# A second attention loop of four units, a ring of two tiles, and operands split first and transposed by DMA

## The reference

```python
x = x + tanh(g_xattn[0]) * xattn0(layernorm(x), ctx)   # 8 heads of 64
x = x + tanh(g_ffn[0])   * expert_choice(layernorm(x)) # 16 experts, sinkhorn, top 32 of 64 tokens
x = x + tanh(g_xattn[1]) * xattn1(layernorm(x), ctx)   # 16 heads of 64
x = x + tanh(g_ffn[1])   * routed(layernorm(x))        # top 2 of 8 experts by each row's first token

def xattn(x, context):
    q, k, v = x @ Wq, context @ Wk, context @ Wv       # split into heads
    attn = softmax(einsum('bhsd,bhld->bhsl', q, k) * 64 ** -0.5)
    return einsum('bhsl,bhld->bhsd', attn, v) @ Wo + bo
```

## Time and profile before

| | us |
|---|---|
| median of 3 runs | 2118.46 (2116.81 to 2119.19) |
| profiled execution, its own time | 2109.9 |
| its span | 2108.1 |
| first attention, first to last projection of queries | 18.9 to 337.4 |
| selection | 355.6 to 486.0 |
| experts | 487 to 1325.4 |
| second attention, first to last projection of queries | 1331.6 to 1968.7 |
| routed layer | 1992.4 to 2108.1 |

### The profile page before, as it was taken

How to read it: one execution, slowest core, us unless ns; L and a number is a source line. 1 busy time by engine, 2 the same in 40 slices (tenths; PEclk the granted TensorE clock), 3 DMA queues, 4 the chain that set the end, 5 groups by cost and what they waited for, 6 DMA issues and landing times. The chain is left out here.

```text
span 2108.1 us, 97301 instructions
## 1 busy us (share of the span) xinstructions
PE 1857.5 (88%) x40785; PEld 1450.6 (69%) x40785; DVE 1582.0 (75%) x3646; ACT 1541.3 (73%) x2701; POOL 671.8 (32%) x920
## 2 busy tenths in 40 slices
PE   5899997877999999999999999687878878889898
PEld 4788886533666666666666676676767767778687
DVE  6899987697888888888888877666656656666654
ACT  4688885666999998989898988466656656677543
POOL 4687776321000000000000000344444444444555
PEclk9999998996999999999999999799989989999899
DMA  6644444591000000000000010366556555533233
GB/s 167 116 94 92 90 95 90 189 368 47 12 15 13 14 12 14 12 14 12 14 14 14 9 48 2 80 112 123 123 96 120 114 108 108 115 72 61 64 106 115
DMA packets 313482, 162.50 MB, mean 77 GB/s; under 512 B 236686, under 2 KB 295990, under 8 KB 313142
## 3 DMA queue, kind: packets, MB, share of 16 engines
q1 hardware_dynamic: 312294, 156.77, 32.5%
q10 hardware_dynamic: 848, 0.71, 0.2%
HBM read 62.07 MB, written 36.57 MB: 47 GB/s over the span
## 5 line engine op out<-in xcount | busy, mean ns | idle before, releaser
L1655 DVE TENSOR_TENSOR h<-g,h 128x1024 f16<-128x1024 f32 x256 | 313.5, 1225 | 138.3 <-ACT h L1587 137.7
L244 PEld LDWEIGHTS psE<-ew,h 128*128 128x128 f16 x6144 | 351.0, 98 | 55.9 <-issue 40.1
L244 PE MATMUL psE<-ew,h 128*128 128x128 f16 x6144 | 365.1, 219 | 12.8 <-DVE eo L1665 6.0
L1582 ACT ACTIVATE g<-psH,eb1T 128x512 f32<-128x512 f32 x512 | 330.3, 680 | 30.9 <-PE psH L244 24.5
L751 POOL TENSOR_TENSOR Ph<-E,Ph 128x512 f16<-128x512 f32 x192 | 222.5, 1159 | 355.0 <-ACT Ph L671 355.0
L671 ACT ACTIVATE QK<-psQK 128x512 f32<-128x512 f32 x216 | 128.8, 596 | 223.9 <-PE psQK L554 223.8
L1587 ACT ACTIVATE h<-g 128x1024 f16<-128x1024 f32 x256 | 270.6, 1057 | 8.1
L1728 POOL MEMSET rbias<- 64x384 f32 x1 | 0.4, 411 | 840.3 <-POOLq L133 840.3
L793 DVE TENSOR_TENSOR vB<-psV,vB 128x512 f16<-128x512 f32 x192 | 132.5, 690 | 157.3 <-ACT vB L671 155.6
L732 POOL TENSOR_TENSOR E<-E,rden 128x512 f32<-128x512 f32 x192 | 200.1, 1042 | 74.6 <-DVE rden L781 74.1
L244 PE MATMUL psH<-shared,ew 128*128 128x512 f16 x768 | 178.9, 383 | 0.0
(11 more groups left out here) (286 smaller groups left out, 3884.8 us busy)
## 6 DMA issues: line engine op xcount, KB each, us to landing
keys_ahead<-shared SPq DMA_DIRECT2D x52, 512.0 KB, 4.8
shared<-keys_ahead SPq DMA_DIRECT2D x52, 512.0 KB, 3.7
rawe<-in_L_ffn_w_dram SPq DMA_DIRECT2D x32, 256.0 KB, 3.1
wb<-rw SPq DMA_DIRECT2D x64, 128.0 KB, 2.0
rows<-places SPq DMA_DIRECT2D x110, 64.0 KB, 2.6
out_dram<-x SPq DMA_DIRECT2D x7, 512.0 KB, 3.3
context_T<-shared SPq DMA_DIRECT2D x64, 48.0 KB, 2.3
PT<-Ph SPq DMA_TRANSPOSE x192, 3.1
```

Source lines behind the costliest of these rows:

```text
L244: last = e.matmul(to, a, b, start=start and n == 0, stop=stop and n == 2, **flags)
L1582: e.activation(g32[:, ft, :], psH[:, ft, :], ACT.Gelu_apprx_tanh, bias=b1T[:, a.expert(1) * FT + ft:a.expert(1) * FT + ft + 1]).then_inc(s ...
L1655: e.tensor_tensor(h[:, 1 - par, 1, 2 * q:2 * q + 2, :], g32[:, 2 * q:2 * q + 2, :], h[:, 1 - par, 0, 2 * q:2 * q + 2, :], ALU.subtract)\
```

## The change

It does six things:

1. The split comes before the transpose. ACT writes `xn` and its float16 high part into `parted`, DVE the rest. In the first attention DVE also writes the context's high part there and POOL its rest. One DMA transpose, issued by SP two steps ahead (`transpose_tokens`), brings all blocks into `XT`: four blocks of 128x128 float16 a unit in the first attention, two a tile (every second step) in the second. PE's two kinds of transposes, their PSUM bank, and their copies are gone.
2. The freed bank makes `psQK` two banks. In the first attention each part has its own, and ACT copies out both parts; in the second the banks alternate from unit to unit. PE's order is now: part 0, part 1, values, `psY`, `psO`, scores.
3. Values are formed for unit j - 2 (was j - 3), with four buffers of `vB` (were two).
4. The second attention's ring of context tiles is two (was four), and the loop body of all engines is four steps (was eight).
5. The keys of all 64 tiles are formed in the selection (`GROUPS` = 16), which starts with them two steps earlier (`FROM` = 4). The branch that formed keys in the second attention is gone.
6. At the end of the expert layer, tile 0 is normalised, split (ACT, POOL) and transposed by DMA.

```diff
-    cT1 = shared[0:DC, 64 * P:72 * P].rearrange("p (r h t) -> p r h t", r=4, h=2)
+    cT1 = shared[0:DC, 64 * P:68 * P].rearrange("p (r h t) -> p r h t", r=2, h=2)
+    XT1 = shared[:, 68 * P:72 * P].rearrange("p (s h t) -> p s h t", s=2, h=2)
...
-            psQK = ps(c, "psQK", [P, 512], F32)
+            psQK = ps(c, "psQK", [P, 2, 512], F32)
...
-            psXC = ps(c, "psXC", [P, 512], F32)
...
-                    pipeline(eng, body, -1, 2 * AHEAD, lo, 2 * AHEAD, RING * G)
-                    pipeline(eng, body, 2 * AHEAD, last, 2 * AHEAD + 8, hi, RING * G)
...
# SP
-                        if nx.opens and not first and nx.ahead:
+                        if nx.opens and not first and nx.j.off > 0:
                             load_keys(e, nx)
+                            load_context(e, nx)
                         if a2.on:
                             wait(e, s["plo"], a2.j)
                             wait(e, s["O"], a2.j - 2)
                             e.dma_start_transpose(PT[:, a2.par].rearrange("p h k t -> p (h k) t"),
                                                   Ph[:, a2.par].rearrange("p h k t -> p (h k t)"))\
                              .then_inc(s[f"pt{a2.par}"], 16)
+                        if soon.opens and (first or soon.j.off > 0):
+                            transpose_tokens(e, soon)
...
+                    def transpose_tokens(e, a):
+                        wait(e, s["xl"], a.t)
+                        if first:
+                            e.wait_ge(s["pad"], 1)
+                            wait(e, s["clo"], a.t)
+                            wait(e, s["V"], a.j - SLOTS)
+                            on_slot(e, "stored", a, -1)
+                        else:
+                            wait(e, s["U0"], a.j - 3)
+                        e.dma_start_transpose(XT[:, a.slot], parted[:, a.slot]).then_inc(s[f"xc{a.slot}"], 16)
...
# PE
-                            pairs = range(4) if a.ahead else range(2 * part, 2 * part + 2)
-                            todo = [(wq, xT[:, a.tp], k) for k in pairs]
-                            if not a.ahead:
-                                todo += [(wk, cT[:, a.ring], k) for k in pairs]
+                            if first:
+                                pairs = range(2 * part, 2 * part + 2)
+                                todo = [(wq, P, k, XT[:, a.slot, 0:2]) for k in pairs] \
+                                    + [(wk, DC, k, XT[0:DC, a.slot, 2:4]) for k in pairs]
+                                bank = part
+                            else:
+                                todo = [(wq, P, k, XT[:, a.slot]) for k in range(4)]
+                                bank = a.par
...
                             if a.opens:
-                                wait(e, s["xh"], a.t)
-                                wait(e, s["xl"], a.t)
...
+                                on_slot(e, "xc", a)
+                            for part in range(2 if first else 1):
+                                wait(e, s[f"uc{part}"], a.j - (1 if first else 2))
+                                project(part)
+                        if a2.on:
...
+                            wait(e, s["vl"], a2.j - 1)
...
-                            for m in range(2):
-                                last = e.matmul(psX[half(m)], xn[:, nx.tp, half(m)], ident32[:], start=True, stop=True)
...
-                            for hl in range(2):
-                                for m in range(2):
-                                    last = e.transpose(psC[half(m), hl, :], cc[:, nx.tp, hl, half(m)], ident16[:])
...
+                    pipeline(e, body, 0, U, 8, U, 4)
...
# ACT
                         if a1.on:
                             wait(e, s["sub"], a1.j)
                             e.activation(E[:, a1.four], E[:, a1.four], ACT.Exp, bias=zero_col[:], scale=DH ** -0.5)\
                              .then_inc(s["exp"], 1)
-                        if a.on and not a.ahead and not first:
-                            projected(e, a, 1, copy)
+                        if a.on and first:
+                            projected(1)
...
-                            copy(cT[:, nx.ring], psC[0:DC]).then_inc(s["ct"], 1)
...
+                        if later.opens:
+                            wait(e, s["xl"], later.t - 2)
+                            e.activation(xn[:, later.tp, :], tile_of(later.t, x), ACT.Identity, bias=column_of(later.t, nmr),
+                                         scale=column_of(later.t, rstd)).then_inc(s["ln"], 1)
+                            on_slot(e, "xc", later, -1)
+                            wait(e, s["ln"], later.t)
+                            copy(parted[:, later.slot, 0, :], xn[:, later.tp, :]).then_inc(s["xh"], 1)
...
# DVE
-                            e.tensor_tensor(xT[:, nx.tp, 1, :], psX, xT[:, nx.tp, 0, :], ALU.subtract)\
-                             .then_inc(s["xl"], 1)
-                        if first and a.on:
-                            projected(e, a, 1, e.tensor_copy)
+                        if soon.opens and (first or soon.j.reg is not None or soon.j.off > 0):
+                            wait(e, s["xh"], soon.t)
+                            e.tensor_tensor(parted[:, soon.slot, 1, :], xn[:, soon.tp, :], parted[:, soon.slot, 0, :],
+                                            ALU.subtract).then_inc(s["xl"], 1)
+                        if first and later.on:
+                            on_slot(e, "xc", later, -1)
+                            e.tensor_copy(parted[:, later.slot, 2, 0:DC], tile_of(later.t, ctx32)).then_inc(s["chi"], 1)
...
# selection
-            GROUPS = AHEAD // 4
-            FROM, EACH = 6, 2
+            GROUPS = NT // 4
+            FROM, EACH = 4, 2
...
# end of the expert layer: SP, ACT, POOL
+                    e.wait_ge(s["lo0"], 1)
+                    e.dma_start_transpose(XT1[:, 0], parted1[:, 0]).then_inc(s["next"], 16)
...
+                    e.activation(parted1[:, 0, 0, :], xna1[:, 0, :], ACT.Copy).then_inc(s["hi0"], 1)
...
+                    e.tensor_tensor(parted1[:, 0, 1, :], xna1[:, 0, :], parted1[:, 0, 0, :], ALU.subtract).then_inc(s["lo0"], 1)
```

More of the change, by code:

```diff
@@ L29 @@
 NE1, TOPK = 8, 2
-AHEAD = 52
 EPS = 1e-5
@@ L433, in __init__, with context, turn_of, on_slot @@
                     self.t, self.tp = self.j.div(G), (self.j.mod(2 * G) // G) % 2
-                    self.ring = (self.j.mod(RING * G) // G) % RING
                     self.opens, self.closes = self.on and self.g == 0, self.on and self.g == G - 1
[L436 to L446, removed]
-                return (t - slot).div(n)
[L450 to L454, removed]
-                    pipeline(eng, body, -1, 2 * AHEAD, lo, 2 * AHEAD, RING * G)
-                    pipeline(eng, body, 2 * AHEAD, last, 2 * AHEAD + 8, hi, RING * G)
+                    self.slot = self.four if first else self.tp
+                def context(self, hl):
+                    return XT[0:DC, self.slot, 2 + hl] if first else cT1[:, self.tp, hl]
+            def turn_of(t, n, slot):
+                return (t - slot).div(n)
+            def on_slot(e, name, a, count=0):
+                wait(e, s[f"{name}{a.slot}"], turn_of(a.t, SLOTS, a.slot) + count, 16)
             with nc.Block() as block:
@@ L522, in _ @@
                     if not first:
-                        e.sem_inc(s["ctx0"], 16)
-                        e.sem_inc(s["ul0"], 16)
-                    for j in range(U + 2):
+                        for name in ("ctx0", "ul0", "xc0"):
+                            e.sem_inc(s[name], 16)
+                    for j in range(-2 if first else 0, U + 2):
                         body(Step(None, 0, j))
@@ L642, in body @@
                             last.then_inc(s["S"], 1)
-                    if first:
-                        pipeline(e, body, -1, U + 5, 8, U - 1, 4)
-                    else:
-                        phases(e, body, U, 8, U - 1)
-                        for j in range(U, U + 5):
-                            body(Step(None, 0, j))
+                    pipeline(e, body, 0, U, 8, U, 4)
+                    for j in range(U, U + 5):
+                        body(Step(None, 0, j))
+                        if not first:
                             if j == U + 1:
@@ L667, in body, with projected @@
                     def body(j):
-                        a, a1, a2, a3, a5, nx, fut = (Unit(j, k) for k in (0, 1, 2, 3, 5, -1, -2))
+                        a, a1, a2, a5, later = (Unit(j, k) for k in (0, 1, 2, 5, -3))
                         def copy(to, frm):
                             return e.activation(to, frm, ACT.Copy)
+                        def projected(part):
+                            wait(e, s["S"], a.j - 2)
+                            wait(e, s[f"U{part}"], a.j)
+                            if first:
+                                to = QK[:, a.par, :, 2 * part:2 * part + 2].rearrange("p q k t -> p q (k t)")
```

(8 more changed lines are left out.)

200 lines of the change are left out of this document (81 added, 119 removed).

## The result

| | us |
|---|---|
| kernel before, beside it on the same chip | 2117.64 (2114.74 to 2119.19, 4 runs) |
| changed kernel | 2044.11 (2039.25 to 2049.63, 4 runs) |
| ratio | 0.9655, 95% interval 0.9628 to 0.9682 |
| profiled execution of the changed kernel, its span | 2044.66, 2042.9 |

The account below looks back on a forecast made before the run. TensorE bound the first attention; in the second no engine was full, and TensorE's eight-step loop body was fetched anew each turn. Terms -101 + 13 + 2 + 11 + 1 = -74 us took 2118.5 to 2044, range 1935 to 2125.

Parts of the forecast that it names:

- The stall goes (part 4): Second attention: TensorE's four-step body stays loaded, so fetch stalls vanish; some 3.65 us a unit if nothing else came late.
- rival C: Second attention: the smaller body still misses at each of 30 turns, 5.1 us each; +79 us, 2198; chance 0.03.
- The token copy is late next: Second attention: token transpose issued behind `PT` sets a two-step loop of 8.37 us, 4.19 a unit; -101 us.
- rest of part 4: Second attention's ring of two: keys and context land with a margin of 1 us or more; 0 (0 to +10).
- First attention, +13: First attention: the same token loop, two steps in 10.02 us, 5.01 a unit against 4.80; +13 us (-1 to +40).
- The start, +2: Before the first unit: the DMA transpose adds about 2 us once (0 to +3).
- Selection and seam, +12: Selection: more key copies, +11 us (+5 to +18); seam after the expert layer: +1 (-2 to +4).
- Two banks, values a step earlier, 0: Both attentions: two banks for `psQK` and earlier values with four buffers cost and bring nothing, 0 (-3 to +3).
- A: Both attentions: token copies hidden, engines bind at 3.65 us a unit in the second, about 4.3 first; 1930; chance 0.13.
- B: Both attentions: token copy backs up behind `PT`, landing in 3.7 and 4.3 us; +59 us, 2178; chance 0.13.
- D: Second attention: PE's new wait every second step lowers its clock; +73 us there, 2117; chance 0.05.
- The Trainium skill's fixed 2.0 us: Token copy's landing: by this fixed DMA cost alone about 2.1 us, second attention 4.04 us a unit, 19 us better.

Follow-up runs that it names:

- experiment 5: Kernel before with only TensorE's loop body in the second attention cut to four steps for the 104 units with keys formed ahead: 1970.78 us, ratio 0.9383.
- 1: Changed kernel with TensorE's loop body in the second attention put back to eight steps: 2174.35 us, ratio 1.0281 to the kernel before.
- 4: Changed kernel with tokens' transpose ahead of `PT` and TensorE's body back to eight, both in the second attention: 2130.82 us, ratio 1.0115 to the kernel before.
- experiment 3: Changed kernel with ACT copying part 1 directly behind part 0 in the first attention: 2037.45 us, ratio 0.9646 to the kernel before.
- experiments 8: Changed kernel with part 1's copy, POOL's context rest, all tokens' transposes, first token transposes and split-weight stores moved earlier: 1945.58 us, ratio 0.926; again 1945.67, 0.9235.
- 9: Kernel with all orders moved, plus the context's high part written by ACT instead of DVE in the first attention: 1941.97 us, ratio 0.9217 to the kernel before.
- experiment 2: Changed kernel with SP issuing the tokens' transpose ahead of `PT` in the second attention: 1979.34 us, ratio 0.9377 to the kernel before.

## Why the prediction was right

What carries the sum was right in mechanism and in size: the stall goes, and the token copy is the limit that comes in its place. That the median fell on 2044 to the microsecond is luck: the profiled executions differ by 65.2 where the sum had 74, and beside experiment 5 the medians differ by 61.9.

- **The stall goes (part 4).** Shown by 1, 4 and 5. Its worth was never a term of the sum, which put a new limit in place of the old. The prediction counted it too low where it did appear: in rival C a turn was 5.1 us, and a turn of eight steps measures 8.9 to 10.5. It also said that between turns PE runs without a gap. That held for the step of the earlier trace rows and not for the body: the 26.4 us before `psO` in the earlier trace rows were quoted and then left out.
- **The token copy is late next, 4.19 us a unit.** Right in each link: issue 5.97 (5.96), L 2.4 (2.39), two steps 8.37 (8.35), stage -101 (-96.7). The 4.4 us between are about what two executions of the changed kernel differ by (540.4 and 536.5). Waits for keys, 7.5 us in 400, are there too, and the step "rest of part 4" had 0 to 10 for them.
- **First attention, +13.** Measured +9.4. The loop that was counted exists, link by link, and has that length (5.04, experiment 3), but a second loop of the same length, ACT's copy of part 1 into the scores, was overlooked. The step placed this copy between exp and `Ph` and followed it only towards `Ph`, not towards `psS`. The number came out right because the two loops agree, not because only one was there.
- **The start, +2.** The step that failed: +7.1. It counted the DMA and not the queue it is put behind, though the gate query's load alone keeps SP for 3.46 us at that place. The DMA itself costs little there: issued first, it lets PE start at 19.2 us (19.2 to 21.4 in experiments 8 and 9), where PE's own transposes had 18.9. Undoing it brings 2.4 us of the 6.8 back, so its price in the total is nearer to the forecast than the row.
- **Selection and seam, +12.** Measured +13.2, and the agreement is luck in part. Up to the first issue behind the selection it is +16.4, where the forecast had +11 (in its range of 5 to 18); the seam gives -3.2 where it had +1 (-2 to +4), and -0.5 in the pair of experiment 5. The copies (+14.6 for 16) and the path behind them (-6.5 for -5.5) came as counted; the +8.3 before the copies was a term that the sum did not have. The pace of the copies is the DMA's: both kernels move 386 to 392 GB/s there.
- **Two banks, values a step earlier, 0.** Nothing in the waits speaks against it. They were not tried by themselves.
- **Rivals.** A's second attention (3.65 a unit) was one SP order away (3.70, experiment 2); its first attention (4.3) was not reached, 296.5 / 64 = 4.63 at best. Landings near B's 3.7 us were seen only beside the instruction fetch (3.5). C falls by the 4 packets, D by the 0.86 us behind a gap of 1.17. The Trainium skill's fixed 2.0 us ("DMA: Bandwidth & Descriptors", Anatomy of one DMA) is given in that section for DMAs that GpSimd issues, and SP issues these. It stands beside landings of 2.3 us here; by the prediction's estimate from it the second attention would have taken 4.04 us a unit, and 4.22 was measured. Of its two rules on fetching ("Runtime: NRT & Kernel Launch", Instruction fetch mechanics), the store of 2048 instructions agrees with what was seen: a body of some 1056 matmuls and loads does not miss, and one of twice that size does.

## What to carry to other kernels

A change of several parts can win by one of them while the others lose: do each part alone before all are kept, above all the one that takes out the largest wait. Of two DMAs that an engine issues in one step, the one whose result is needed first belongs ahead in its program: here both feed step J + 2, the tokens at its start and `PT` only for its `psO`. Where one wait ends last, look for a second loop of the same length behind it before its removal is counted as a gain.

## What the runs showed of the hardware

- A loop body that is brought in anew costs more than the stall at its head: PE also stops within the body, in the middle of a set of matmuls, some 8.3 us of waits a turn for 10 packets (0.17 MB), and at a mean granted clock of 0.93 instead of 1.00 (experiments 4 and 2, 1400 to 1800).
- Issuing a DMA transpose kept SP for 1.20 us with two blocks (one `shared<-shared` at 1609.80) and 1.24 with eight (`PT` in the first attention); in landing they differ, 2.3 against 2.7 (experiment 5) to 3.7 us (the changed kernel).
- The landing of both kinds grew beside the fetch of instructions where PE waited for it (5.2 and 3.5 us in experiment 1), but not in experiment 4 (3.0 and 2.3). Why they differ stays open.
